# Second attention layer: one transpose of the keys per head, and two ScalarE copies in place of the other

## The chip, the cores and the metric

The kernel runs on one core of one Trainium2 chip. The metric is the device time of one execution in microseconds (us). A core has five engines that run at the same time and wait for each other by semaphores: TensorE (PE in the profile, PEld for its weight loads), VectorE (DVE), ScalarE (ACT), GpSimd (POOL) and SyncE (SP). Each engine works through its own instructions strictly in order. TensorE writes its results to PSUM, eight banks of 128 partitions by 512 float32 columns; the other engines copy them from there to SBUF.

## The reference, cut to what matters

The model is two pre-norm transformer layers on 8 sequences of 512 tokens, width 256. The change lies in the attention of the second layer (L1), which has 16 heads of width 64:

```python
x = x + L0_attn(layernorm(x))
x = x + L0_ffn(layernorm(x))        # mixture of 8 experts
x = x + L1_attn(layernorm(x))       # <- the change is in here
x = x + L1_ffn(layernorm(x))        # fp4-quantised weights and inputs

def _L1_attn_ref(x, W_in, b_in, W_out, b_out):
    proj = x @ W_in.T + b_in                 # q, k, v: 16 heads x 64 each
    q, k = _rope(q, sin, cos), _rope(k, sin, cos)
    att = einsum('bhqd,bhkd->bhqk', q, k) * (1 / sqrt(64))
    att = softmax(where(causal, att, -inf))
    y = einsum('bhqk,bhkd->bhqd', att, v)
    return y @ W_out.T + b_out
```

## The kernel before

L1's attention runs one batch (one sequence of 512 tokens) after the other, eight in all, and in a batch one head after the other. A head's scores are 512 by 512 and causal, so only ten of its sixteen 128x128 tiles are computed. They fall into three groups: the query tiles 0 and 1 (128 and 256 key columns), query tile 2 (384) and query tile 3 (512). One group is one **slot** of the program; slot k of a batch belongs to head k // 3 and group k % 3, so a batch has 48 slots. In this text "the first exponential of a head" is that of its slot 3h, and "the 512-column scores" are those of its slot 3h+2.

Each engine's program is written slot by slot, with a fixed order of parts in a slot and fixed lags in slots behind the scores:

- TensorE (order S, T, P, F): the scores of slot k (S), the transposes of the probabilities of slot k-2 (T), their product with the values of slot k-4 (P), then the fills (F): all work that goes into the two PSUM banks named `W`.
- ScalarE (order P, H, W, E): rounding of projected pieces to float16 (lines 483 to 493), `p_hi`, the float16 half of the transposed probabilities of slot k-2 (H, line 442), copies out of the `W` banks (W, line 453 for the stack, 458 and 474 for others), and at the end the exponential of slot k (E, line 434).
- VectorE (order O, L, W, M, N): head outputs, `p_lo` of slot k-3 (line 538, needs `p_hi`), the projected pieces out of the `W` banks (`t_buf`, line 579, and `rope_u`, line 586), the row maxima of slot k (M, line 531), and the next batch's layer norm.
- GpSimd: the rest of the rotary embedding and the low float16 half of q, k and v (lines 707 to 726).

The scores need float32-like precision, so q and k are each split into a high and a low float16 half of 64 columns, stored side by side in `q_stage` and `k_stage`. Transposed, a query tile has q_hi on partitions 0 to 63 and q_lo on 64 to 127. One matmul against [k_hi; k_lo] gives hi*hi + lo*lo; a second one, against [k_lo; k_hi], gives the cross terms. Both keys' arrangements live in `stack`, 128 partitions by three times 512 columns for each of two heads: queries, keys, keys with their halves swapped. To make the swapped one, `k_stage` holds the high half twice (hi, lo, hi; lines 492 and 493), and TensorE transposes columns 64 to 191 as well.

So the stack of the next head is filled in two parts, `FILLS = 2`. In slot 3h TensorE transposes four query and four key tiles into one `W` bank (line 342), and ScalarE copies 128x1024 out (line 453). In slot 3h+1 TensorE transposes the four swapped key tiles into the other `W` bank, and ScalarE copies 128x512.

The other fills share the two `W` banks in strict turn: 24 pieces of the projection of the next heads (line 371, six matmuls of 512 columns each), four transposes of x, eight of the head outputs (yT), four output projections (proj, float32). A fill waits until the fill two places back has been copied out. Tables give the slots, for instance:

```python
AT_1 = (1, 2, 4, 6, 8, 12, 14, 15, 16, 18, 19, 21)     # pieces, second half of the heads
AT_0 = (24, 26, 28, 30, 33, 34, 36, 38, 39, 40, 42, 43)  # pieces, the next batch's first half
```

The scores of slot k wait for the exponential of slot k-2 (`s_exp`, the two score banks take turns), and those of a head's first slot also for its stack (`s_stev`).

Of the kernel before, what the change touches and what calls it, by code (L numbers as in the profile page):

```python
# [9 lines left out]
ACT = mybir.ActivationFunctionType  # L10
# [4 lines left out]
P = 128  # L15
B, T, D = 8, 512, 256
# [15 lines left out]
K0 = TERMS0 + 8  # L32
# [82 lines left out]
def attention(block, layer, x_sb, stats, consts, w, sem, sb, banks, aside=None):  # L115
# [10 lines left out]
    L1 = layer == 1  # L126
# [9 lines left out]
    DH = DH1 if L1 else DH0  # L136
    HC = P // DH
    CHUNKS = HEADS // HC
    FILLS = 2 if L1 else 1
    QW = 128 if L1 else K0  # L140
    KW = 192 if L1 else K0
    VW = 130 if L1 else 51
    OW = 65 if L1 else 51
    PIECES = 12 if L1 else 4
    S, PT, W, ob = banks[0:2], banks[2:4], banks[5:7], (banks[4], banks[7])
    LOW = F16 if L1 else BF16
# [3 lines left out]
    q_stage = sb(f"q_stage{layer}", [P, 2, QT, 8, QW], LOW)  # L150
    k_stage = sb(f"k_stage{layer}", [P, 2, QT, 8, KW], LOW)
    v_stage = sb(f"v_stage{layer}", [P, 2, QT, 8, VW], LOW)
    stack = sb(f"stack{layer}", [P, 2, (1 + FILLS) * T], LOW)
    xn = sb(f"xn{layer}", [P, 2, D], F32)
    xnT = sb(f"xnT{layer}", [P, 2, C, T] if L1 else [P, C, T], F16 if L1 else F32)
    prob = [sb(f"prob{layer}_{g}", [P, n], F32) for g, n in enumerate(GROUP_COLS)]
# [30 lines left out]
    s_stev = sem("stack_ready")  # L187
# [4 lines left out]
    s_ph = sem("piece_hi_ready")  # L192
# [76 lines left out]
    def _(pe):  # L269
# [57 lines left out]
        def fill(cur, off, kind, *a):  # L327
            b = cur + off
            bank, _ = work_banks.next(kind)
# [4 lines left out]
            if kind == "stack":  # L334
                h, r = a
                if h % 8 == 0 and r == 0:
                    wait(pe, s_piece, (2 * b + h // 8) * PIECES + (8 if L1 else PIECES))
                rows = P if L1 else K0
                pairs = [(q_stage, 0, 0), (k_stage, 0, T)] if r == 0 else [(k_stage, 64, 0)]
                for stage, c0, col in pairs:  # L340
                    for j in range(QT):
                        last = pe.transpose(out.bitcast(LOW)[0:rows, col + j * P:col + (j + 1) * P],  # L342
                                            stage[:, h // 8, j, h % 8, c0:c0 + rows], ident_l[:, :])
                last.then_inc(s_st, 1)
                taken[bank] = (s_stev, FILLS * HEADS, off, FILLS * h + r + 1)
                return
            if kind == "xT":
                j, = a
# [9 lines left out]
            elif kind == "piece":  # L358
                half, p = a
# [64 lines left out]
    def _(act):  # L424
# [19 lines left out]
        def take(kind, b, *a):  # L444
            bank, n = work_banks.next(kind)
            if kind == "stack":
# [1 line left out]
                wait(act, s_st, FILLS * (b * HEADS + h) + r + 1)  # L448
                wait(act, s_scores, 3 * (b * HEADS + h - 1))
                rows = P if L1 else K0  # L450
                dst = stack[0:rows, h % 2, 0:2 * T] if r == 0 else stack[0:rows, h % 2, 2 * T:3 * T]
                src = W[bank][:, :].bitcast(LOW)[0:rows, 0:2 * T if r == 0 else T]
                act.activation(dst, src, ACT.Copy).then_inc(s_stev, 1)  # L453
            elif kind == "xT":
                j, = a
                wait(act, s_fill, n)
# [19 lines left out]
        def piece_hi(b, half, p):  # L476

            m = b * 2 * PIECES + half * PIECES + p
            t, j = piece_parts(p)
            if t == 2:  # L480
                wait(act, s_taken, m + 1)
                wait(act, s_pv, 3 * (b * HEADS - HEADS + 8 * half + 8))
                act.activation(v_stage[:, half, j, :, 0:64], t_buf[:, p % 4, :].rearrange("p (h d) -> p h d", d=64),
                               ACT.Copy).then_inc(s_ph, 1)
                return
            wait(act, s_z, b * 16 + 8 * half + p + 1)
            wait(act, s_st, FILLS * (b * HEADS - HEADS + 8 * half + 8))
            z = rope_z[:, p % 2, :, :]
            if t == 0:
                act.activation(q_stage[:, half, j, :, 0:64], z, ACT.Copy).then_inc(s_ph, 1)  # L490
            else:
                act.activation(k_stage[:, half, j, :, 0:64], z, ACT.Copy)
                act.activation(k_stage[:, half, j, :, 128:192], z, ACT.Copy).then_inc(s_ph, 1)

        def prologue():
            for j in range(QT):
# [2019 lines left out]
```

## Time and profile before

| | |
|---|---|
| median of 3 runs | 2277.01 us (2276.40 to 2287.38) |
| the profiled execution | 2284.02 us, span 2282.2 us |
| mean granted TensorE clock | 0.941 |
| busy: PE, PEld, DVE, ACT, POOL | 1963.1, 1402.1, 1723.2, 1400.1, 1025.3 us |
| prologue and eight batches of L1's attention | about 925 to 1970 us of the span |
| first scores of the eight batches | 970.68, 1109.71, 1233.55, 1355.39, 1477.24, 1599.08, 1720.94, 1843.62 us |

The profile is one execution; its times are not means over runs. A row of the timeline gives the start of an instruction in us from the start of the span, its duration in us, the engine, the line of the kernel, what is written and read, and in brackets how long the engine had been idle before it and what ended the wait. A batch of the middle takes about 121.85 us, and batches 2 to 5 (counted from 0) repeat each other to some hundredths of a microsecond. The worked example of the prediction is batch 3.

### The profile page before, as it was taken

To read this page: it belongs to the slowest core of one execution; us is meant where nothing else is said; L and a number is where in the kernel's file an instruction comes from. 1 tells how busy PE (TensorE), PEld (TensorE's weight loads), DVE (VectorE), ACT (ScalarE), POOL (GpSimd) and SP (SyncE) were. 2 spreads that over 40 slices of the span, in tenths; PEclk is the share of its full clock that TensorE was granted. 3 is DMA by queue.
4 is the path that set the end of the run, shared out by engine and by line. 5 is a ranking of instruction groups with operands and counts; after the bars stand their busy time and mean duration, and the time that the engine had idled before them with its cause. 6 is when DMAs were issued, how large, how long until landed. Compare 5 with 4: busy or idle time off the path is not lost. (4 is left out here: it accounts for less than half of the span.)

```text
span 2282.2 us, 52729 instructions
## 1 busy us (share of the span) xinstructions
PE 1963.1 (86%) x18758; PEld 1402.1 (61%) x18759; DVE 1723.2 (76%) x3728; ACT 1400.1 (61%) x2750; POOL 1025.3 (45%) x1207
## 2 busy tenths in 40 slices
PE   6988999889825996487899999999999999459999
PEld 4666666666623664165677777777767677336665
DVE  8878888888772443487688887878797968679997
ACT  4666666666642443286678786969687879244343
POOL 5434454343032001689757475757675753132222
PEclk9999999999757998799999999999999999769999
DMA  7000000000153332012100000000000000100000
GB/s 245 2 2 2 2 1 2 2 1 2 32 180 90 87 93 62 1 18 36 15 2 2 2 2 1 2 1 2 1 2 2 2 2 2 39 1 16 16 18 24
DMA packets 53369, 57.77 MB, mean 25 GB/s; under 512 B 7104, under 2 KB 47376, under 8 KB 53152
## 3 DMA queue, kind: packets, MB, share of 16 engines
q1 hardware_dynamic: 46528, 45.79, 6.3%
q0 software_dynamic: 6416, 8.95, 1.9%
q8 instruction: 139, 2.28, 0.4%
q14 instruction: 78, 0.64, 0.1%
q10 hardware_dynamic: 208, 0.11, 0.0%
HBM read 36.22 MB, written 18.61 MB: 24 GB/s over the span
## 5 line engine op out<-in xcount | busy, mean ns | idle before, releaser
L371 PE MATMUL a_bank<-w_in_sb,xnT_sb 128*128 128x512 f16 x1152 | 288.6, 389 | 33.8 <-DVE t_buf_sb L579 28.1
L531 DVE TENSOR_REDUCE neg_max_sb<-a_bank 128x1 f32<-128x128 f32 (+3 forms) x512 | 236.0, 482 | 91.4 <-PE a_bank L288 90.0
L1209 DVE TENSOR_REDUCE neg_max_sb<-a_bank 128x1 f32<-128x128 f32 (+3 forms) x512 | 235.9, 484 | 81.7 <-PE a_bank L938 77.6
L1098 ACT ACTIVATE probT_sb<-a_bank 128x512 f32<-128x512 f32 (+1 forms) x384 | 198.7, 526 | 144.4 <-PE a_bank L961 139.5
L442 ACT ACTIVATE p_hi_sb<-a_bank 128x384 f16<-128x384 f32 (+1 forms) x384 | 204.9, 534 | 120.9 <-PE a_bank L297 119.2
L434 ACT ACTIVATE prob_sb<-a_bank,neg_max_sb 128x128 f32<-128x128 f32 (+3 forms) x512 | 260.8, 542 | 22.7 <-DVE neg_max_sb L531 21.8
L538 DVE TENSOR_TENSOR p_lo_sb<-a_bank,p_hi_sb 128x384 f16<-128x384 f32 (+1 forms) x384 | 227.9, 595 | 60.7 <-ACT p_hi_sb L442 57.0
L453 ACT ACTIVATE stack_sb<-a_bank 128x1024 f16<-128x1024 f16 (+1 forms) x256 | 211.1, 825 | 7.1 <-PE a_bank L342 6.7
L297 PE MATMUL a_bank<-ident_f_sb,prob_sb 128*128 128x128 f32 x1280 | 206.9, 277 | 3.7 <-DVE p_lo_sb L538 3.1
L707 POOL TENSOR_TENSOR rope_w_sb<-t_buf_sb,sin_sb 128x256 f32<-128x256 f32 x128 | 146.4, 1144 | 134.6 <-DVE t_buf_sb L579 132.4
L371 PEld LDWEIGHTS a_bank<-w_in_sb,xnT_sb 128*128 128x128 f16 x1152 | 104.1, 99 | 140.6 <-DVE t_buf_sb L579 35.9
L283 PE MATMUL a_bank<-stack_sb 128*128 128x128 f16 (+3 forms) x512 | 148.6, 303 | 26.1 <-ACT prob_sb L434 22.8
L713 POOL TENSOR_TENSOR rope_z_sb<-rope_u_sb,rope_w_sb 128x512 f32<-128x512 f32 x128 | 163.4, 1277 | 10.0
L1396 POOL TENSOR_TENSOR parts_sb<-rest_sb,one_sb 128x256 bf16<-128x256 f32 x60 | 36.7, 612 | 278.2 <-DVE rest_sb L1240 278.2
L318 PE MATMUL a_bank<-v_stage_sb,p_hi_sb 128*128 128x65 f16 x1280 | 159.4, 197 | 0.0
L317 PE MATMUL a_bank<-v_stage_sb,p_hi_sb 128*128 128x65 f16 x1280 | 158.4, 194 | 0.7 <-DVE p_lo_sb L538 0.6
L319 PE MATMUL a_bank<-v_stage_sb,p_lo_sb 128*128 128x65 f16 x1280 | 157.5, 193 | 0.0
L579 DVE SCALAR_TENSOR_TENSOR t_buf_sb<-a_bank,bias_sb 128x512 f32<-128x512 f32 x192 | 131.6, 686 | 33.1 <-PE a_bank L371 21.1
L284 PE MATMUL a_bank<-stack_sb 128*128 128x128 f16 (+3 forms) x512 | 155.0, 303 | 0.0
L297 PEld LDWEIGHTS a_bank<-ident_f_sb,prob_sb 128*128 128x128 f32 x1280 | 135.4, 142 | 30.1 <-issue 4.2
L937 PE MATMUL a_bank<-stack_sb 104*128 104x128 bf16 (+3 forms) x512 | 143.6, 307 | 5.3 <-DVE neg_max_sb L1209 2.9
L2394 POOL TENSOR_TENSOR pair_q_sb<-pair_quot_sb,pair_scale_sb 128x960 f32<-128x960 f32 (+2 forms) x36 | 59.1, 1641 | 197.2 <-DVE pair_quot_sb L2379 197.2
(272 smaller groups left out, 5608.5 us busy)
## 6 DMA issues: line engine op xcount, KB each, us to landing
sorted_rows<-zeros_sb SPq DMA_DIRECT2D x1, 4992.0 KB, 22.7
x_in_sb<-sorted_rows SPq DMA_DIRECT2D x39, 128.0 KB, 2.2
sorted_results<-y_moe_sb SPq DMA_DIRECT2D x39, 128.0 KB, 1.7
x_sb_sb<-L_attn_x SPq DMA_DIRECT2D x8, 512.0 KB, 9.7
w_raw_sb<-L_ffn_gate_bank SPq DMA_DIRECT2D x8, 512.0 KB, 3.8
w_raw_sb<-L_ffn_up_bank SPq DMA_DIRECT2D x8, 512.0 KB, 4.8
w_raw_sb<-L_ffn_down_bank SPq DMA_DIRECT2D x8, 512.0 KB, 5.8
out<-x_sb_sb SPq DMA_DIRECT2D x32, 128.0 KB, 1.7
```

Of the source, the lines that this page charges most:

```text
L297: last = pe.transpose(PT[G_BANK(h, g)][:, n * P:(n + 1) * P], prob[g][:, n * P:(n + 1) * P], ident_f[:, :])
L317: pe.matmul(o, hi, v[:, 0:65], start=a, stop=False)
L318: pe.matmul(o, hi, v[:, 65:130], start=False, stop=False)
L371: last = pe.matmul(out, xnT[:, x, c, j * P:(j + 1) * P], w["in"][:, w_, c, cols], start=k == 0, stop=k == len(terms) - 1)
L434: last = act.activation(prob[g][:, off:off + L], S[(3 * h + g) % 2][:, off:off + L], ACT.Exp, bias=neg_max[:, i:i + 1])
L442: act.activation(p_hi[g][:, h % 2, :], PT[G_BANK(h, g)][:, 0:GROUP_COLS[g]], ACT.Copy).then_inc(s_hi, 1)
L453: act.activation(dst, src, ACT.Copy).then_inc(s_stev, 1)
L531: last = dve.tensor_reduce(neg_max[:, i:i + 1], S[(3 * h + g) % 2][:, off:off + L], AX.X, ALU.max, negate=True)
L538: dve.tensor_tensor(p_lo[g][:, h % 2, :], PT[G_BANK(h, g)][:, 0:GROUP_COLS[g]], p_hi[g][:, h % 2, :], ALU.subtract).then_inc(s_lo, 1)
L713: pool.tensor_tensor(rope_z[:, p % 2, :, :], rope_u[:, p % 2, :, :], rope_w[:, :, :], ALU.add).then_inc(s_z, 1)
L1098: act.activation(probT[:, (h // 4) % 2, h % 4, T_AT[r]:T_AT[r + 1]], ST[(3 * h + r) % 2][:, 0:T_AT[r + 1] - T_AT[r]], ACT.Exp).then_inc(s_ ...
L1209: last = dve.tensor_reduce(neg_max[:, h % 2, i:i + 1], S[(3 * h + g) % 2][:, off:off + L], AX.X, ALU.max, negate=True)
```

## The change

The swapped keys are no longer transposed. `FILLS` becomes 1: TensorE fills one `W` bank per head, and ScalarE copies three times out of it: the 128x1024 copy as before, and then the transposed keys again by 64 partitions, partitions 0 to 63 of PSUM to partitions 64 to 127 of the third part of `stack`, and 64 to 127 to 0 to 63. The third copy releases the stack. `k_stage` is 128 columns wide in place of 192, and its second copy of the high half (line 493) is gone.

```diff
-    FILLS = 2 if L1 else 1
+    FILLS = 1
     QW = 128 if L1 else K0
-    KW = 192 if L1 else K0
+    KW = 128 if L1 else K0
...
-    stack = sb(f"stack{layer}", [P, 2, (1 + FILLS) * T], LOW)
+    stack = sb(f"stack{layer}", [P, 2, (3 if L1 else 2) * T], LOW)
...
                 rows = P if L1 else K0
-                pairs = [(q_stage, 0, 0), (k_stage, 0, T)] if r == 0 else [(k_stage, 64, 0)]
-                for stage, c0, col in pairs:
+                for stage, c0, col in ((q_stage, 0, 0), (k_stage, 0, T)):
                     for j in range(QT):
                         last = pe.transpose(out.bitcast(LOW)[0:rows, col + j * P:col + (j + 1) * P],
...
                 rows = P if L1 else K0
-                dst = stack[0:rows, h % 2, 0:2 * T] if r == 0 else stack[0:rows, h % 2, 2 * T:3 * T]
-                src = W[bank][:, :].bitcast(LOW)[0:rows, 0:2 * T if r == 0 else T]
-                act.activation(dst, src, ACT.Copy).then_inc(s_stev, 1)
+                src = W[bank][:, :].bitcast(LOW)
+                last = act.activation(stack[0:rows, h % 2, 0:2 * T], src[0:rows, 0:2 * T], ACT.Copy)
+                if L1:
+
+                    for a in range(2):
+                        last = act.activation(stack[64 - 64 * a:128 - 64 * a, h % 2, 2 * T:3 * T],
+                                              src[64 * a:64 * a + 64, T:2 * T], ACT.Copy)
+                last.then_inc(s_stev, 1)
...
-                act.activation(k_stage[:, half, j, :, 0:64], z, ACT.Copy)
-                act.activation(k_stage[:, half, j, :, 128:192], z, ACT.Copy).then_inc(s_ph, 1)
+                act.activation(k_stage[:, half, j, :, 0:64], z, ACT.Copy).then_inc(s_ph, 1)
```

On ScalarE, this is what stands from slot 27 to slot 29 of a middle batch (head 9) in the kernel before: the stack copy (L453), the two exponentials of the slot (L434), `p_hi` (L442), the second stack copy, and so on to the exponential of the 512-column slot.

```order
L453 ACTIVATE stack_sb<-a_bank 128x1024
L434 ACTIVATE prob_0_sb<-a_bank,neg_max_sb 128x128
L434 ACTIVATE prob_0_sb<-a_bank,neg_max_sb 128x256
L442 ACTIVATE p_hi_2_sb<-a_bank 128x512
L453 ACTIVATE stack_sb<-a_bank 128x512
L434 ACTIVATE prob_1_sb<-a_bank,neg_max_sb 128x384
L492 ACTIVATE k_stage_sb<-rope_z_sb 128x8x64
L493 ACTIVATE k_stage_sb<-rope_z_sb 128x8x64
L442 ACTIVATE p_hi_0_sb<-a_bank 128x384
L474 ACTIVATE yT_sb<-a_bank 128x512
L434 ACTIVATE prob_2_sb<-a_bank,neg_max_sb 128x512
```

The same place in the changed kernel, whose line numbers differ by a few:

```order
L451 ACTIVATE stack_sb<-a_bank 128x1024
L455 ACTIVATE stack_sb<-a_bank 64x512 x2
L433 ACTIVATE prob_0_sb<-a_bank,neg_max_sb 128x128
L433 ACTIVATE prob_0_sb<-a_bank,neg_max_sb 128x256
L441 ACTIVATE p_hi_2_sb<-a_bank 128x512
L433 ACTIVATE prob_1_sb<-a_bank,neg_max_sb 128x384
L496 ACTIVATE k_stage_sb<-rope_z_sb 128x8x64
L441 ACTIVATE p_hi_0_sb<-a_bank 128x384
L478 ACTIVATE yT_sb<-a_bank 128x512
L433 ACTIVATE prob_2_sb<-a_bank,neg_max_sb 128x512
```

Two copies of 64 partitions now stand ahead of the head's first exponential, the 128x512 copy behind it is gone, and so is the second copy of the key piece.

On TensorE, this is the end of slot 28 and the start of slot 29 in the kernel before: the product with the values (L317 to L319), the four swapped key transposes (L342), a piece of the projection (L371), and the 512-column scores (L283).

```order
L317 MATMUL a_bank<-v_stage_sb,p_hi_0_sb 128x65
L318 MATMUL a_bank<-v_stage_sb,p_hi_0_sb 128x65
L319 MATMUL a_bank<-v_stage_sb,p_lo_0_sb 128x65
L342 MATMUL a_bank<-ident_h_sb,k_stage_sb 128x128 x4
L371 MATMUL a_bank<-w_in_sb,xnT_sb 128x512 x6
L283 MATMUL a_bank<-stack_sb 128x512
```

And in the changed kernel:

```order
L317 MATMUL a_bank<-v_stage_sb,p_hi_0_sb 128x65
L318 MATMUL a_bank<-v_stage_sb,p_hi_0_sb 128x65
L319 MATMUL a_bank<-v_stage_sb,p_lo_0_sb 128x65
L370 MATMUL a_bank<-w_in_sb,xnT_sb 128x512 x6
L283 MATMUL a_bank<-stack_sb 128x512
```

Four transposes are gone between the slot's last product and its piece; nothing else moves on TensorE, and VectorE's and GpSimd's instructions keep their order.

## Rows read from the trace of the kernel before

**Rows 1.** Busy time by stretch: stretch, length, busy us of each engine, clock, DMA.

```profile
1300.00:1400.00 100.00, 97.01 (x1059) 74.44 (x1060) 78.80 (x167) 78.69 (x154) 64.13 (x61) 1.00 0.01 2
```

**Rows 2.** Groups by line and shape: count, busy us, mean ns, idle before.

```profile
L453 ACT ACTIVATE stack_sb<-a_bank 128x1024 f16<-128x1024 f16 x128 | 132.0, 1031 | 7.1 <-PE a_bank L342 6.7
...
L342 PE MATMUL a_bank<-ident_h_sb,k_stage_sb 128*128 128x128 f16 x1024 | 100.3, 221 | 7.4 <-ACT stack_sb L453 7.3
...
L726 POOL TENSOR_TENSOR k_stage_sb<-rope_z_sb,k_stage_sb 128x512 f16<-128x512 f32 x64 | 80.2, 1253 | 11.3 <-ACT k_stage_sb L493 9.8
...
L493 ACT ACTIVATE k_stage_sb<-rope_z_sb 128x512 f16<-128x512 f32 x64 | 40.3, 630 | 0.0
...
L1103 ACT ACTIVATE stack_sb<-a_bank 2x512 bf16<-2x512 f32 x64 | 37.7, 589 | 19.2 <-PE a_bank L947 15.6
```

**Rows 3.** Timeline of TensorE, batch 3, head 9, slots 28 and 29.

```profile
1434.47 0.39 PE L342 MATMUL a_bank<-ident_h_sb,k_stage_sb 128*128 128x128 f16 x4
1434.69 1.46 PE L371 MATMUL a_bank<-w_in_sb,xnT_sb 128*128 128x512 f16 x6
1435.99 0.38 PE L283 MATMUL a_bank<-stack_sb 128*128 128x512 f16 x1
```

**Rows 4.** Timeline of ScalarE, batch 3, slots 27 to 30.

```profile
1433.57 1.02 ACT L453 ACTIVATE stack_sb<-a_bank 128x1024 f16<-128x1024 f16 x1 [0.25 <-PE a_bank L342]
1434.49 0.72 ACT L434 ACTIVATE prob_sb<-a_bank,neg_max_sb 128x128 f32<-128x128 f32 x2
1435.09 0.61 ACT L442 ACTIVATE p_hi_sb<-a_bank 128x512 f16<-128x512 f32 x1
1435.57 0.62 ACT L453 ACTIVATE stack_sb<-a_bank 128x512 f16<-128x512 f16 x1
1436.05 0.61 ACT L434 ACTIVATE prob_sb<-a_bank,neg_max_sb 128x384 f32<-128x384 f32 x1
...
1438.40 0.74 ACT L434 ACTIVATE prob_sb<-a_bank,neg_max_sb 128x512 f32<-128x512 f32 x1
...
1439.35 1.08 ACT L453 ACTIVATE stack_sb<-a_bank 128x1024 f16<-128x1024 f16 x1
```

**Rows 5.** Timeline of VectorE, batch 3, slots 28 and 29.

```profile
1435.73 0.69 DVE L538 TENSOR_TENSOR p_lo_sb<-a_bank,p_hi_sb 128x512 f16<-128x512 f32 x1 [0.34 <-ACT p_hi_sb L442]
1436.34 0.68 DVE L579 SCALAR_TENSOR_TENSOR t_buf_sb<-a_bank,bias_sb 128x512 f32<-128x512 f32 x1
1437.05 0.69 DVE L586 TENSOR_TENSOR rope_u_sb<-t_buf_sb,cos_sb 128x512 f32<-128x512 f32 x1
1437.66 0.68 DVE L531 TENSOR_REDUCE neg_max_sb<-a_bank 128x1 f32<-128x512 f32 x1
```

**Rows 6.** Timeline, batch 3: first exponential, then 512-column scores, of heads 8 and 10.

```profile
1428.42 0.74 ACT L434 ACTIVATE prob_sb<-a_bank,neg_max_sb 128x128 f32<-128x128 f32 x2
1429.37 0.38 PE L283 MATMUL a_bank<-stack_sb 128*128 128x512 f16 x1
...
1440.27 0.78 ACT L434 ACTIVATE prob_sb<-a_bank,neg_max_sb 128x128 f32<-128x128 f32 x2
...
1441.77 0.38 PE L283 MATMUL a_bank<-stack_sb 128*128 128x512 f16 x1
```

**Rows 7.** The same pair of heads 12 and 13 of batch 3.

```profile
1454.35 0.74 ACT L434 ACTIVATE prob_sb<-a_bank,neg_max_sb 128x128 f32<-128x128 f32 x2
...
1455.15 0.39 PE L283 MATMUL a_bank<-stack_sb 128*128 128x512 f16 x1 [0.23 <-ACT prob_sb L434]
...
1460.47 0.73 ACT L434 ACTIVATE prob_sb<-a_bank,neg_max_sb 128x128 f32<-128x128 f32 x2
...
1463.41 0.38 PE L283 MATMUL a_bank<-stack_sb 128*128 128x512 f16 x1
```

**Rows 8.** The same pair of head 14 of the last batch.

```profile
1936.78 0.73 ACT L434 ACTIVATE prob_sb<-a_bank,neg_max_sb 128x128 f32<-128x128 f32 x2
...
1937.56 0.39 PE L283 MATMUL a_bank<-stack_sb 128*128 128x512 f16 x1 [0.41 <-ACT prob_sb L434]
```

## The prediction

> **What bounds the kernel now.** I read the busy times by stretch first. In the steady batches TensorE is busy 97.0 of 100 us at the full granted clock, VectorE 78.8, ScalarE 78.7 and GpSimd 64.1 [rows 1]. So TensorE looks like the bound, and work taken off it looks like a gain; but a busy share tells nothing of who waits in a loop. Next I read the timeline of one head on three engines [rows 3 to 5]. TensorE's own work of head 9, from its 512-column scores (1435.99) to those of head 10 (1441.77), takes 5.78 us [rows 3, 6]. The same 5.78 us is the distance of the two stack copies on ScalarE, 1433.57 and 1439.35 [rows 4]. The way between these copies is an unbroken chain over two engines: stack copy 1433.57, exponentials 1434.49, `p_hi` 1435.09, then VectorE's `p_lo` at 1435.73, which had waited 0.34 us for `p_hi`, the piece out of its bank 1436.34, the rotary product 1437.05, the row maximum 1437.66, then back to ScalarE's exponential at 1438.40 and, two instructions later, the next stack copy [rows 4, 5]. In a head with little projection work this loop is as long as TensorE's work: ScalarE and VectorE have slack on average, but not on this path.
>
> Third, the distance from the end of a head's first exponential to the 512-column scores that need it. Heads 8, 9, 10 and 12 have 0.21, 0.78, 0.72 and 0.06 us (1428.42 + 0.74 = 1429.16 against 1429.37, and so on), head 13 has 2.21 [rows 3, 4, 6, 7]. It must be at least 0.06, as where TensorE is shown to wait for it [rows 7]. The long ones have two pieces of projection, or an output projection, between the stack's fill and these scores; the short ones have one piece or none.
>
> **The change part by part.** *TensorE* loses four transposes a head, 512 of the 1024 in the key group [rows 2]. The group of four starts at 1434.47 and the next work at 1434.69: 0.22 us [rows 3] (the busy times of single matmuls overlap and can't be added). For 128 heads that is 28.2 us, if TensorE is the bound at each.
>
> *ScalarE* gains two 64x512 copies ahead of the first exponential and loses the 128x512 copy behind `p_hi`. No row shows a copy from one half of the partitions to the other. The nearest, 128x512 from the same bank, takes 0.48 us from its start to that of the next instruction (1435.57 to 1436.05) [rows 4]; the 128x1024 copy takes 0.92 (1433.57 to 1434.49) [rows 4]. Whether half the rows halve the price is answered best by a copy of 2 partitions by 512, whose mean is 589 ns, against 619 for the 128x512 copy at 1435.57 [rows 2, 4]: rows hardly count. I take 0.5 us for each, 1.0 for both. Bounds: 0.25 each if rows did count, 0.62 each if the copies did not overlap at all.
>
> The Trainium skill, page "ScalarE: Activation LUTs", section "What ACT_TABLE_LOAD costs", has one element per cycle and lane, 186 ns + 0.833 ns for each element of the row, and 93 ns of overlap; by it the estimate is 1.04 us for both copies, and no less for half the partitions. By that the sum below would stand about 2 us higher; the two-partition row agrees with it.
>
> *The first exponential ends 1.0 us later.* Behind it on ScalarE are `p_hi` of the slot before, the exponentials of the head's other two slots, and rounding of pieces; TensorE's 512-column scores wait for it. Where the distance is over 1.0 + 0.06, nothing is lost and the 0.22 is won. Where it is d, the scores come 1.0 - (d - 0.06) later: 0.28 in head 9, 0.85 in head 8, 1.0 in head 12.
>
> *The loop.* `p_hi` is delayed by the same 1.0 us, and the removed copy stands behind it, so it gives nothing back here. In head 9, `p_lo`, piece, rotary product, maximum and the last exponential follow without a gap [rows 5], so the next stack copy starts 1.0 later, and with its own two small copies head 10's first exponential ends 2.0 later. Its distance is 0.72: head 10's 512-column scores are 1.34 late, of which 0.28 were counted in head 9. With 0.08 more at the next wait this makes 1.14 for head 10.
>
> *One batch.* I went through the 16 heads of batch 3 in this way, starting at head 4, since the output projections before it leave ScalarE idle and reset the loop. Gain or loss of each in us: head 4 +0.28, 5 -0.22, 6 and 7 +0.07 together (VectorE is busy without a gap there on the next batch's layer norm and sets the pace), 8 +0.84, 9 +0.28, 10 +1.14, 11 +0.05, 12 +0.83, 13 -0.39, 14 +0.04, 15 +1.20, then head 0 +0.11, 1 +0.37, 2 +0.88 (the late maximum delays the copy of yT, whose bank a piece waits for), 3 -0.42. The larger gains of 13 and 3 are bank waits that go, since one fill a head less takes its turn. The losers sum to +6.09, the winners to -1.03: **+5.1 us a batch**.
>
> *The second copy of the key pieces* (630 ns [rows 2]) goes; in the steady batches ScalarE's next instruction mostly waits for TensorE or VectorE anyway, so I give it nothing there; were that cover gone, 64 copies at 0.52 would be worth up to 33 us. In the prologue GpSimd waits for it (9.8 us in all behind line 493 [rows 2]): four pieces at about 0.52 make -2.1, and the extra copy before the first scores +0.5: -1.6.
>
> *The sum.* Six middle batches: 6 x 5.1 = 30.6. First batch: its second half like the others +4, its first half, where GpSimd sets part of the pace, an estimate of +2: 6. Last batch: its second half has no projection work, the scores wait for the first exponential in each head (1936.78 + 0.73 = 1937.51 against 1937.56 [rows 8]); seven heads lose between 0.5 (ScalarE's net work) and 1.0, I take 0.7, 4.9; its first half 1.9. Together 30.6 + 6 + 6.8 - 1.6 = **+41.8 us** on the profiled execution's 2284.0, so 2325.8. That execution stands 7.0 us above the median of the runs, so on the median's scale 2277.0 + 41.8 = **2319 us**, 1.8% slower.
>
> **The rivals.** All on the median's scale.
>
> *A: the copies are hidden everywhere.* Then -28.2 - 1.6: 2247 us. For it: TensorE's 97.0 against ScalarE's 78.7. Against: the distances of 0.06 to 0.78. It decides below about 0.4 us for both copies, where the ledger's losers sink to the size of the winners. [...]
>
> *B: the wait is direct only.* If VectorE takes the late `p_lo` in its stride, the heads lose only what the first wait costs: in the ledger +1.9 a batch, 11.4 for six, with 6 for the first and last together less 1.6: 2293 us. For it: VectorE's 78.8. Against: the gapless rows of head 9.
>
> *C: the loop closes in every head.* Each pays 1.0 - 0.22: 128 x 0.78 = 100, 2377 us. Against: head 13's 2.21 us and the idle ScalarE during the output projections.
>
> *D: a copy of half the partitions takes half the time.* The exponential is 0.5 late, ScalarE's net work is zero, and the ledger nearly cancels, about +0.7 a batch: 2283 us with the ends. Against: the 2-partition row.
>
> **How the numbers follow.** Chances: forecast 0.50, B 0.20, C (or most of it) 0.10, D 0.12, A 0.08. The predicted time is the forecast's. Copies of 0.62 us each would add about 0.24 at nine losing heads, 2 us a batch, 16 in all; errors of the ledger of 2 us a batch are as much: 2300 to 2337 for the forecast alone. The range reaches from D, 2283, to 2352, where it leaves out A and the upper part of C. About 0.5% (11.4 us) is what a measurement of this kernel can tell from no change. Forecast, B and C are slower than that: 0.80. D is within: 0.12. A is faster: 0.08.
>
> **What would show it.** Right: small copies that start 0.5 us apart; the first exponential's end to the 512-column scores at 0.06 in heads 8, 9, 10, 12, 15 and all heads of the last batch's second half; a distance about 1.2 us smaller in the long heads; middle batches of about 127 us against 121.85; TensorE's busy share down, and its idle time ahead of the scores put down to the exponential; GpSimd no longer waiting behind line 493. Wrong: middle batches under 121 us (A), of 122 to 124 (B, D), with the spacing of the small copies telling D from B, or above 130 (C).

## The result and the profile after

The changed kernel took 2359.68 us (median of four runs, 2355.82 to 2362.29) against 2277.85 for the kernel before on the same chip (2276.40 to 2287.38): ratio 1.0329, 95% interval 1.0300 to 1.0358. It is slower, by 82 us where 42 were forecast. All ratios here are of fast runs; one of the ten runs of e2 took 3973.93 us and is not in its ratio. The profiled execution took 2362.29 us with a span of 2360.5; its span is 78.3 above that of before, and the numbers below are read from these two traces.

The period of a batch, from the first scores of one batch to those of the next, shows where the time went. Before, the seven periods were 139.03, 123.84, 121.84, 121.85, 121.85, 121.85 and 122.69 us; after, 142.98, 133.45, 131.53, 131.68, 131.53, 132.12 and 131.71. From the last batch's first scores to the start of the feed-forward part it took 133.18, now 150.50. So the first batch lost 3.9, the six middle ones 58.1 together, the last 17.3; 1.6 were won ahead of the first scores.

Busy time by stretch, in the columns of [rows 1], the same 100 us:

```profile
1300.00:1400.00 100.00, 84.27 (x946) 61.83 (x943) 79.85 (x165) 85.49 (x161) 62.77 (x60) 1.00 0.01 2
```

These 100 us are less than a batch and hold other heads of it in each kernel, so 97.0 and 84.3 can't be compared. Here is a whole batch, batch 3, first before, then after:

```profile
1355.39:1477.24 121.85, 116.38 (x1281) 88.42 (x1282) 99.89 (x209) 96.61 (x189) 77.21 (x72) 1.00 0.01 2
...
1377.01:1508.69 131.68, 116.51 (x1219) 86.88 (x1218) 101.23 (x210) 105.17 (x197) 77.43 (x73) 0.98 0.01 2
```

TensorE has fallen from 95.5% of the batch to 88.5%, VectorE from 82.0 to 76.9, and ScalarE went from 79.3 to 79.9. No engine is nearer its limit than before, and TensorE is still the busiest. Something that no busy share shows, a chain over several engines, sets the pace.

The groups that answer to [rows 2], whole span:

```profile
L455 ACT ACTIVATE stack_sb<-a_bank 64x512 f16<-64x512 f16 x256 | 151.5, 592 | 3.0
...
L451 ACT ACTIVATE stack_sb<-a_bank 128x1024 f16<-128x1024 f16 x128 | 131.2, 1025 | 15.1 <-PE a_bank L341 14.5
...
L729 POOL TENSOR_TENSOR k_stage_sb<-rope_z_sb,k_stage_sb 128x512 f16<-128x512 f32 x64 | 80.3, 1254 | 10.3 <-ACT k_stage_sb L496 10.3
...
L341 PE MATMUL a_bank<-ident_h_sb,k_stage_sb 128*128 128x128 f16 x512 | 52.2, 227 | 0.0
```

Half the key transposes are gone. A copy of half the rows lasts 592 ns, against 619 for the 128x512 copy of before. GpSimd still waits 10.3 us behind the copy of the key pieces.

The two ends of the loop, as in [rows 4, 5]: head 9 of batch 3 on ScalarE, then on VectorE.

```profile
1459.72 1.02 ACT L451 ACTIVATE stack_sb<-a_bank 128x1024 f16<-128x1024 f16 x1 [0.33 <-PE a_bank L341]
1460.76 1.20 ACT L455 ACTIVATE stack_sb<-a_bank 64x512 f16<-64x512 f16 x2
1461.98 0.73 ACT L433 ACTIVATE prob_sb<-a_bank,neg_max_sb 128x128 f32<-128x128 f32 x2
1462.60 0.60 ACT L441 ACTIVATE p_hi_sb<-a_bank 128x512 f16<-128x512 f32 x1
...
1465.88 0.69 ACT L433 ACTIVATE prob_sb<-a_bank,neg_max_sb 128x512 f32<-128x512 f32 x1 [0.74 <-DVE neg_max_sb L534]
...
1466.84 1.03 ACT L451 ACTIVATE stack_sb<-a_bank 128x1024 f16<-128x1024 f16 x1
```

```profile
1463.23 0.69 DVE L541 TENSOR_TENSOR p_lo_sb<-a_bank,p_hi_sb 128x512 f16<-128x512 f32 x1 [1.68 <-ACT p_hi_sb L441]
1463.84 0.68 DVE L582 SCALAR_TENSOR_TENSOR t_buf_sb<-a_bank,bias_sb 128x512 f32<-128x512 f32 x1
1464.56 0.69 DVE L589 TENSOR_TENSOR rope_u_sb<-t_buf_sb,cos_sb 128x512 f32<-128x512 f32 x1
1465.16 0.68 DVE L534 TENSOR_REDUCE neg_max_sb<-a_bank 128x1 f32<-128x512 f32 x1
```

From the 128x1024 copy to the first exponential it is 2.26 us, where [rows 4] have 0.92: 1.34 more. From one stack copy to the next it is 7.12, where it was 5.78: 1.34 more. In this head the whole delay goes round the loop once and comes out at its end. VectorE's wait for `p_hi` has grown from 0.34 to 1.68, by 1.34 again, and behind it the four instructions follow each other as before.

What TensorE and VectorE waited for between 1250 and 1850 us (line waited for: us in total, times, longest):

```profile
PE a_bank L283 <- ACT prob_sb L433: 37.1, 42, 2.5
...
PE a_bank L370 <- ACT stack_sb L455: 5.8, 13, 0.6
...
DVE p_lo_sb L541 <- ACT p_hi_sb L441: 65.2, 56, 2.9
```

In the same stretch before, TensorE's wait for the exponential was 6.6 us in 20 times, and VectorE's for `p_hi` 23.8. The second row is new: the matmuls of a piece need the bank that the third copy releases.

First exponential and 512-column scores, as in [rows 3, 7, 8]: head 9 of batch 3 by the exponential above (1461.98 + 0.73 = 1462.71, scores at 1462.77), then heads 8 of batch 3 and 14 of the last batch.

```profile
1454.73 0.73 ACT L433 ACTIVATE prob_sb<-a_bank,neg_max_sb 128x128 f32<-128x128 f32 x2
1455.52 0.39 PE L283 MATMUL a_bank<-stack_sb 128*128 128x512 f16 x1 [1.25 <-ACT prob_sb L433]
...
2018.39 0.73 ACT L433 ACTIVATE prob_sb<-a_bank,neg_max_sb 128x128 f32<-128x128 f32 x2
...
2019.18 0.39 PE L283 MATMUL a_bank<-stack_sb 128*128 128x512 f16 x1 [1.98 <-ACT prob_sb L433]
```

The distance is 0.06 in both, with TensorE idle for 1.25 and 1.98 us before it.

### The profile page after: what moved, and what is told of

Read it like the earlier page. It is cut to its first block and busy times, and to the rows that moved or that the text cites. A ratio compares the mean times of both kernels' runs of the same rounds, so it can differ in the third digit from the quotient of the medians.

```text
span 2360.5 us, 51642 instructions
## 1 busy us (share of the span) xinstructions
PE 1962.3 (83%) x18246; PEld 1389.1 (59%) x18247; DVE 1730.3 (73%) x3728; ACT 1468.8 (62%) x2814; POOL 1025.7 (43%) x1207
## 5 line engine op out<-in xcount | busy, mean ns | idle before, releaser
L370 PE MATMUL a_bank<-w_in_sb,xnT_sb 128*128 128x512 f16 x1152 | 294.0, 394 | 42.2 <-ACT stack_sb L455 17.8
L283 PE MATMUL a_bank<-stack_sb 128*128 128x128 f16 (+3 forms) x512 | 151.0, 307 | 90.5 <-ACT prob_sb L433 87.9
L317 PE MATMUL a_bank<-v_stage_sb,p_hi_sb 128*128 128x65 f16 x1280 | 160.0, 195 | 0.7 <-DVE p_lo_sb L541 0.6
L319 PE MATMUL a_bank<-v_stage_sb,p_lo_sb 128*128 128x65 f16 x1280 | 159.3, 194 | 0.0
L455 ACT ACTIVATE stack_sb<-a_bank 64x512 f16<-64x512 f16 x256 | 151.5, 592 | 3.0
```

Source lines behind the costliest of these rows:

```text
L317: pe.matmul(o, hi, v[:, 0:65], start=a, stop=False)
L319: last = pe.matmul(o, lo, v[:, 0:65], start=False, stop=z)
L370: last = pe.matmul(out, xnT[:, x, c, j * P:(j + 1) * P], w["in"][:, w_, c, cols], start=k == 0, stop=k == len(terms) - 1)
```

## The experiments

Theories. *Loop and price*: the loss is what ScalarE adds between the stack copy and the first exponential, times the heads in which the loop or the direct wait closes. *Direct wait only*: VectorE takes the late `p_hi` in its stride. *Length*: ScalarE's additional microsecond a head costs wherever it stands. *Bank*: the loss is the bank that is held longer. All ratios are to the kernel before, run on the same chip with the kernel named; edits are against the changed kernel. e1, e2 and e3 leave out the product's terms that need the swapped halves of the keys: the stack holds unswapped ones there. One fill fewer for each head, and with it another turn of the two `W` banks, is in all twelve, also in e2 and e7, which are not slower.

**e1: two 128x512 copies.** As long in sum as the ledger assumed, in the same place.

```diff
-                    for a in range(2):
-                        last = act.activation(stack[64 - 64 * a:128 - 64 * a, h % 2, 2 * T:3 * T],
-                                              src[64 * a:64 * a + 64, T:2 * T], ACT.Copy)
+                    act.activation(spare[:, :], src[:, T:2 * T], ACT.Copy)
+                    last = act.activation(stack[:, h % 2, 2 * T:3 * T], src[:, T:2 * T], ACT.Copy)
```

> The two 64-row copies are replaced by two 128x512 copies of the transposed keys (one into a spare tile, one unswapped into the third part of the stack, so the cross terms of the scores are left out). The distance from the start of the 128x1024 copy to that of the first exponential, 0.92 us before and 2.26 us in the changed kernel, should be about 1.9 here. Theory 'price' (the ledger is right, only the two copies cost 1.34 us in place of 1.0): about 2319 us, 2305 to 2333, so half of the loss. Theory 'ledger' (at 1.0 us the loop closes in more heads than I followed): 2340 us or more.

Measured: 2319.45 us, ratio 1.0154 (1.0120 to 1.0188). ScalarE's timeline:

```profile
1461.21 1.02 ACT L452 ACTIVATE stack_sb<-a_bank 128x1024 f16<-128x1024 f16 x1
1462.11 0.61 ACT L455 ACTIVATE spare_sb<-a_bank 128x512 f16<-128x512 f16 x1
1462.59 0.62 ACT L456 ACTIVATE stack_sb<-a_bank 128x512 f16<-128x512 f16 x1
1463.07 0.76 ACT L434 ACTIVATE prob_sb<-a_bank,neg_max_sb 128x128 f32<-128x128 f32 x2
```

Each instruction starts before the one ahead of it has ended, by about 0.13 us: 1.86 from the first to the exponential, 0.94 more than before. Batches 2 to 5 took 126.6 us, 4.7 more than before; the ledger had 5.1 at a price of 1.0. By the ratio e1 is 35 us slower, where the forecast had 42; that its 2319 is also the forecast's number is chance, since the kernel before ran 2286 on this chip.

**e2: one 128x512 copy** in place of the two.

```diff
-                    for a in range(2):
-                        last = act.activation(stack[64 - 64 * a:128 - 64 * a, h % 2, 2 * T:3 * T],
-                                              src[64 * a:64 * a + 64, T:2 * T], ACT.Copy)
+                    last = act.activation(stack[:, h % 2, 2 * T:3 * T], src[:, T:2 * T], ACT.Copy)
```

> One 128x512 copy in place of the two 64-row ones (unswapped, so the cross terms of the scores are left out): 0.5 us ahead of the first exponential, as one copy less behind p_hi. Theory 'price': the losses and gains of the heads nearly cancel, about 2283 us, 2270 to 2295. Theory 'ledger': the losers still lead, 2300 us or more.

Measured: 2284.64 us, ratio 1.0002 (0.9985 to 1.0019); middle batches 122.9. At half the price gain and loss cancel, as rival D had worked out.

**e3: the same halves, not crossing.**

```diff
-                        last = act.activation(stack[64 - 64 * a:128 - 64 * a, h % 2, 2 * T:3 * T],
+                        last = act.activation(stack[64 * a:64 * a + 64, h % 2, 2 * T:3 * T],
```

> The two 64-row copies stay on their own half of the partitions (unswapped, so the cross terms of the scores are left out). If a copy does not overlap its neighbours because it crosses from one half of the partitions to the other: 128x1024 copy to first exponential 1.9 us and about 2319 us. If because its rows start at another partition than its neighbour's: one or two of the three overlaps stay lost, 2.1 to 2.26 us and 2340 to 2360 us.

Measured: 2347.11 us, ratio 1.0271 (1.0235 to 1.0307).

```profile
1457.73 1.02 ACT L451 ACTIVATE stack_sb<-a_bank 128x1024 f16<-128x1024 f16 x1 [0.33 <-PE a_bank L341]
1458.65 1.18 ACT L455 ACTIVATE stack_sb<-a_bank 64x512 f16<-64x512 f16 x2
1459.85 0.73 ACT L433 ACTIVATE prob_sb<-a_bank,neg_max_sb 128x128 f32<-128x128 f32 x2
```

The first copy, which reads and writes the lower half, starts 0.92 behind the stack copy and overlaps it. The pair and the exponential behind it do not overlap (1.18 and 1.20 for the two): 2.12 in all. So of the 0.40 by which the changed kernel's copies cost more than those of e1, 0.26 go with the split into halves and 0.14 with the crossing.

**e4 and e5: the copies later.** In e4 they stand behind the head's first exponentials, ahead of `p_hi`; in e5 behind that `p_hi`. Their source is still the bank, which only the last of them releases.

```diff
+            while held:
+                h, src = held.pop()
+                for a in range(2):
+                    last = act.activation(stack[64 - 64 * a:128 - 64 * a, h % 2, 2 * T:3 * T],
+                                          src[64 * a:64 * a + 64, T:2 * T], ACT.Copy)
+                last.then_inc(s_stev, 1)
```

> The two 64-row copies stand behind the first exponentials of the head instead of ahead of them, still ahead of p_hi. If the direct wait of the 512-column scores for the first exponential makes the loss: about 2255 to 2285 us. If the way over p_hi, p_lo, row maximum and the last exponential to the next stack copy makes it: 2310 us or more, with the scores waiting for the second and third exponential and for the stack.

> The two 64-row copies stand in slot 3h+1 behind p_hi, where the 128x512 copy of the kernel before stood. Neither the first exponential nor p_hi is late then. If the loop over p_hi is what costs (theory 'loop'): most of the loss is gone, 2265 to 2295 us; what is left is that a W bank is held until the third copy, so a piece in slot 3h+1 waits for it. If ScalarE's longer work as such costs (0.7 us a head net): 2330 us or more.

Measured: e4 2354.14 us, ratio 1.0307 (1.0279 to 1.0336); e5 2376.75, ratio 1.0392 (1.0372 to 1.0413). Taking the direct wait of the head's own exponentials away (e4) gives back about 5 us, within the intervals nothing, but the bank is now held longer: TensorE's waits for these copies grew from 6.4 to 26.2 us. The expectation for e5 was missed by 80. Its waits on TensorE, 1250 to 1850 us:

```profile
PE a_bank L370 <- ACT stack_sb L449: 46.7, 35, 1.9
PE a_bank L387 <- ACT stack_sb L449: 16.3, 10, 1.6
```

The wait for the exponential is down from 37.1 to 13.5, but 63 us of waits for the held bank came in its place. Two causes are mixed here, so e9 to e11 separate them.

**e6: four transposes put back** on TensorE (the key's, made a second time into the same place).

```diff
-                for stage, c0, col in ((q_stage, 0, 0), (k_stage, 0, T)):
+                for stage, c0, col in ((q_stage, 0, 0), (k_stage, 0, T)) + (((k_stage, 0, T),) if L1 else ()):
```

> The changed kernel with four more key transposes a head (the transposed keys are written a second time to the same place of the bank), so that TensorE has its old work again. If TensorE's time is no longer on the path where ScalarE's loop sets the pace, at most 12 us above the changed kernel, 2360 to 2372; if it still sets the pace, 28 us more, 2388.

Measured: 2373.61 us, ratio 1.0373 (1.0351 to 1.0396), 0.0044 above the changed kernel's: about 10 us, with 8 either way, by the two intervals. Of the 28.2 us of the saved transposes about a third, by the intervals between 2 and 18 us, still reached the changed kernel's time.

**e7: the halves swapped by two DMAs** from SyncE's queue, so that ScalarE does no swap at all.

```diff
+                for a in range(2):
+                    sp.dma_start(stack[64 - 64 * a:128 - 64 * a, G % 2, 2 * T:3 * T],
+                                 stack[64 * a:64 * a + 64, G % 2, T:2 * T]).then_inc(s_oev, 16)
...
+                    wait(pe, s_oev, 32 * (b * HEADS + h + 1))
```

> The halves are swapped by two DMAs from SBUF to SBUF, issued by SyncE behind the 128x1024 copy, so ScalarE does no small copies and TensorE no second transposes. If the loop through ScalarE set the pace: faster than before, 2250 to 2265 us, if the swapped keys land within the some 3 us that a short head leaves from the end of the copy to the next head's first scores. If they land later, the scores wait for them: 2280 us or more with a wait on a DMA.

Measured: 2272.74 us, ratio 0.9940 (0.9919 to 0.9962): 0.6% faster than the kernel before. On the scale of the expectation (2250 to 2265) the ratio gives 2264. Middle batches 119.3 us. Busy time of one of them:

```profile
1225.47:1344.73 119.26, 112.13 (x1217) 84.94 (x1217) 100.45 (x209) 85.87 (x165) 77.10 (x72) 1.00 0.08 19
```

TensorE is back at 94.0% with the shorter work. The batch is 2.6 us shorter than before: that is what the single transpose is worth once the swap is off the loop, together with the two ScalarE copies, of the stack and of the key piece, that are gone here too; the two were not separated. The DMA issues between 1250 and 1850 us (count, KB each, median us from issue to landing):

```profile
stack_sb<-stack_sb SPq DMA_DIRECT2D x160, 64.0 KB, 2.0
```

Half of them land within 2.0 us of their issue, the slowest took 3.7, and a head lasts about 7. TensorE waited for a landing nine times in this stretch, 4.2 us in all.

**e8: the second copy of the key pieces restored** to the changed kernel.

```diff
+                act.activation(k_stage[:, half, j, :, 128:192], z, ACT.Copy).then_inc(s_ph, 1)
```

> The changed kernel with the second ScalarE copy of the key pieces' high half put back (k_stage of 192 columns, the extra 64 unused). The prediction gave that copy 2.1 us in the prologue and nothing in the batches: 2360 to 2365 us. If ScalarE's work in the loop counts in full, 64 x 0.52 = 33 us more: 2393.

Measured: 2380.14 us, ratio 1.0397 (1.0375 to 1.0419), 0.0068 or about 15 us above the changed kernel, with 8 us either way; middle batches 133.4 against 131.7. That lies between the two expectations. The first and last key piece of the prologue on GpSimd, in the kernel before and in the changed one:

```profile
937.23 1.16 POOL L726 TENSOR_TENSOR k_stage_sb<-rope_z_sb,k_stage_sb 128x512 f16<-128x512 f32 x1 [1.26 <-ACT k_stage_sb L493]
...
966.62 1.16 POOL L726 TENSOR_TENSOR k_stage_sb<-rope_z_sb,k_stage_sb 128x512 f16<-128x512 f32 x1 [1.26 <-ACT k_stage_sb L493]
```

```profile
936.43 1.15 POOL L729 TENSOR_TENSOR k_stage_sb<-rope_z_sb,k_stage_sb 128x512 f16<-128x512 f32 x1 [0.74 <-ACT k_stage_sb L496]
...
964.26 1.15 POOL L729 TENSOR_TENSOR k_stage_sb<-rope_z_sb,k_stage_sb 128x512 f16<-128x512 f32 x1 [0.74 <-ACT k_stage_sb L496]
```

From first to last it is 29.39 and 27.83 us, and 29.41 in e8 (941.08 to 970.49): GpSimd's wait is 0.52 shorter at each piece, and three of them make the 1.56. In the steady batches the removed copies were worth 1.7 us a batch in the changed kernel. The other 4.7 us by which e8's prologue starts later lie ahead of it, in work that the edit doesn't touch.

**e9, e10, e11: place and bank apart.** The copies read the stack, so that the first copy releases the bank by itself; the scores wait for the two copies. e9: behind `p_hi`, where the kernel before had its second stack copy. e10: behind the first exponentials, ahead of `p_hi`. e11: in the changed kernel's own place. The edit of all three; only where `swap()` is called differs:

```diff
+                n, r = held.pop()
+                wait(act, s_stev, n + 1)
+                for a in range(2):
+                    last = act.activation(stack[64 - 64 * a:128 - 64 * a, r, 2 * T:3 * T],
+                                          stack[64 * a:64 * a + 64, r, T:2 * T], ACT.Copy)
+                last.then_inc(s_oev, 1)
...
+                act.activation(stack[0:rows, h % 2, 0:2 * T], src[0:rows, 0:2 * T], ACT.Copy).then_inc(s_stev, 1)
+                held.append((b * HEADS + h, h % 2))
```

> The two 64x512 copies take the first copy's result in the stack as their source and stand behind the first rounding copy in slot 3h+1; the first copy releases the bank by itself and the scores wait for the two copies. Theory loop (the copies cost because they stand between the stack copy, the exponentials and the rounding copy that the key blocks wait for): the loop is that of before, TensorE keeps its 0.22 a head, 2255 to 2290. Rival length (ScalarE 1.3 us longer in each head costs wherever it stands): 2330 or more. If only the held bank cost in the earlier run with this place, the 2377 of that run falls below 2300.

> The same source, the copies behind the first exponentials and ahead of the rounding copy: no wait of the head's own exponentials for them, and no bank held, but the loop keeps them. Theory loop: 2315 to 2345. If the held bank was the cost of the run with this place and the bank as source (2354): 2290 or less.

> The same source in the changed kernel's own place, ahead of the exponentials: loop and direct wait stay, only the bank is free 1.2 us sooner. Theory loop: 2340 to 2365, at most 15 below the changed kernel, since the waits for the bank behind the copies are 5.8 us of 600 there. If the bank was the cost: 2310 or less. If copies that read the stack overlap each other as the 128-row ones do, their price falls towards 1.0 and the time towards 2320.

Measured: e11 2374.79 us, ratio 1.0405 (1.0369 to 1.0441); e10 2343.43, 1.0267 (1.0232 to 1.0303); e9 2299.46, 1.0075 (1.0043 to 1.0107). The same two copies, of the same length, cost 92, 61 or 17 us by the place alone: 31 us go with the direct wait of the head's own exponentials, 44 more with `p_hi`. e9 lies 9 us above its expectation. In e11 nothing was won by the free bank; it fell outside its expectation, on the slow side. ScalarE in e11:

```profile
1384.00 1.02 ACT L463 ACTIVATE stack_sb<-a_bank 128x1024 f16<-128x1024 f16 x1
1385.06 1.27 ACT L451 ACTIVATE stack_sb<-stack_sb 64x512 f16<-64x512 f16 x2
1386.35 0.73 ACT L434 ACTIVATE prob_sb<-a_bank,neg_max_sb 128x128 f32<-128x128 f32 x2
```

Copies out of the stack are longer, and the first of them has to wait for the end of the 128x1024 copy: 2.35 to the exponential, 0.09 above the changed kernel. In e9 the copies are behind `p_hi`, and the second exponential stands behind them:

```profile
1387.96 0.60 ACT L442 ACTIVATE p_hi_sb<-a_bank 128x512 f16<-128x512 f32 x1 [2.79 <-PE a_bank L298]
1388.58 1.27 ACT L451 ACTIVATE stack_sb<-stack_sb 64x512 f16<-64x512 f16 x2
1389.87 0.58 ACT L434 ACTIVATE prob_sb<-a_bank,neg_max_sb 128x384 f32<-128x384 f32 x1
```

**e12: one step further back**, behind the second exponential.

```diff
                     exp(b, k // 3, k % 3)
+                    if L1 and k % 3 == 1:
+                        swap()
```

> The same stack source; the two copies stand one step further back than in e9, behind the head's second exponential (128x384) and ahead of the next rounding copy. Theory loop: like e9 they are outside the loop of stack copy, first exponentials, rounding copy and key blocks, so the time stays far below the changed kernel: 2260 to 2310. What is left in e9 (1.6 a batch above the kernel before) is then put down to the second exponential behind the copies, and goes if it is that alone: 2255 to 2285; it stays or grows (2290 to 2320) if the rounding copy and the third exponential behind the new place are as close to TensorE's wait. Rival length (ScalarE's 1.3 a head costs wherever it stands): 2330 or more.

Measured: 2315.10 us, ratio 1.0130 (1.0092 to 1.0167). Not better than e9: the rest isn't the second exponential alone. TensorE's waits, 1250 to 1850 us:

```profile
PE a_bank L284 <- issue: 21.5, 38, 1.1
...
PE a_bank L284 <- ACT stack_sb L451: 8.9, 5, 1.8
PE a_bank L284 <- ACT prob_sb L434: 5.7, 14, 0.6
```

The wait for the exponential is nearly gone (26.1 us in e9), but the next head's scores now wait for the copies themselves. That is the second row, and the first too, which has no releaser in the view: each of its 38 matmuls starts 0.10 us after the end of a second copy of the pair. Together they make 30.4 us. None of the four places that were tried was free of cost.

**Together.** Added time between the stack copy and the first exponential, and the time of the kernel, with the copies in the changed kernel's place:

```
kernel    added us   ratio    ratio x 2280 us, above before
e2          0.48     1.0002       0
e1          0.94     1.0154     +35
e3          1.20     1.0271     +62
after       1.34     1.0329     +75
e11         1.43     1.0405     +92
```

From e1 to the changed kernel 0.40 us add 40, from e1 to e11 0.49 add 57: 100 to 116 us for one microsecond, with some 25 either way by the intervals. If each of the 128 heads paid all of it, it would be 128. So past about 1 us most heads pay.

## Why the prediction was right or wrong

**The bound.** Right. It was the loop and not TensorE's 97.0% (95.5% over a whole batch). With 28 us of work off TensorE and 1.34 us a head into the loop, all of it showed up at the loop's end in head 9; that [rows 3] and [rows 4] had the same 5.78 was the sign. The Trainium skill's page "Perfetto Trace Analysis", section "Identifying the Most-Contended Engine", says that the busy share of the matmuls is no good measure of how near TensorE is to its limit, and names the share of the peak matmul rate and the busy share of the weight loads in its place. The trace agrees: the engine with 97.0 was relieved and the kernel got slower, and the weight loads had 74.4 in [rows 1], below VectorE's 78.8 and ScalarE's 78.7. A's time came near only when the swap left ScalarE (e7, 2273), and there 13 us were won where A had 30.

**The price of the two copies: here the prediction failed.** The step read "I take 0.5 us for each, 1.0 for both". They cost 1.34, and e1, with copies that cost 0.94 in the same place, lost 35 us in place of 75. The 1.34 come from 1.04 behind the 128x1024 copy (0.92 before), then 0.60 and 0.62. Even the upper bound, 0.62 each, left out that the copy ahead of them loses its own overlap of 0.1. The sources stood in [rows 2, 4]: the row of 2 partitions was read for its duration, and the spacing for the small copies was taken from the 128-row copy, of which 0.13 lies under the next instruction. The start-to-start time of small copies was in the trace of before, in the layer ahead:

```profile
300.28 1.02 ACT L1118 ACTIVATE stack_sb<-a_bank 104x1024 bf16<-104x1024 bf16 x1 [0.59 <-PE a_bank L994]
301.20 0.59 ACT L1098 ACTIVATE probT_sb<-a_bank 128x512 f32<-128x512 f32 x1
...
305.06 0.59 ACT L1103 ACTIVATE stack_sb<-a_bank 2x512 bf16<-2x512 f32 x1 [0.64 <-PE a_bank L947]
305.68 0.87 ACT L1098 ACTIVATE probT_sb<-a_bank 128x512 f32<-128x512 f32 x2
```

The copy of 104 rows from partition 0 gives 0.1 of its time to the next instruction; the copy of 2 rows, which starts at partition 96, gives nothing. The Trainium skill, page "ScalarE: Activation LUTs", section "What ACT_TABLE_LOAD costs", states 93 ns of overlap, by which the estimate was 1.04 for both. e1 comes near it (0.94, with overlaps of 0.11 to 0.14 in its trace); the copies of halves, which didn't overlap, don't.

**What a microsecond in the loop costs: mis-sized too.** "Copies of 0.62 us each would add about 0.24 at nine losing heads", 16 us: 67 for a microsecond. The runs show 100 to 116. At its own 67 the missing 0.34 would have given 23 us more, 2342; the other 18 are this rate. It is higher because more heads than nine lie in the loop once the first 1.0 us has used up their distances, and because the last batch and stretches of lower clock add to it. By head, from the starts of successive 512-column scores in the middle batches, where the clock stayed up: with 0.40 more in the loop than e1, heads 0, 1, 4, 8, 9 and 10 take 0.37 longer each, 7 and 15 0.69 and 0.51, 11, 12 and 14 0.20 to 0.24; only 2, 5 and 13 pay 0.12 or less, and 3 and 6 nothing. Together 4.3 a batch, as much as 11 of the 16 heads paying all of the 0.40.

**The ledger.** Right at its own price. e1 has +4.7 a batch for +5.1. By head it is right in heads 2 to 5 and 9 to 11 (head 9 +0.26 for +0.28, head 10 +0.96 for +1.14, head 3 -0.44 for -0.42). It is wrong by 0.9 too high in heads 6 and 7 together, 1.3 too low in head 8, 0.9 too high in head 0 and 0.5 too low in head 15. These errors cancel, so it is in part luck that the sum of the batch came out.

**Middle batches.** 58.1 for 30.6. The higher price accounts for those 4.3 a batch, 26 us, less the 0.4 a batch by which the ledger was too high. The rest, some 4 us, goes with the granted clock, which the prediction took as constant: in three of the batches head 0 took 1.3 to 1.4 longer than in the others, behind a stretch of lower clock.

**First batch and prologue.** 3.9 for an estimate of 6. The prologue's parts were right: on GpSimd it takes 34.5 us from the start of the first query piece (932.11) to that of the last key piece (966.62) before and 32.4 after (931.83 to 964.26), so four pieces gave the 2.1 of the forecast. From there to the first scores it takes 0.7 longer, for +0.5. The total of -1.6 agrees, with 0.3 won ahead of these pieces; by itself it would show little, since the first scores start anywhere from 961 to 975 in the traces of the twelve experiments.

**Last batch.** 17.3 for 6.8. The distances of 0.06 came in each head from 7 to 14, as forecast; the price was 0.9 to 1.6 a head for 0.7, and two heads lost 3.0 and 2.5. From one head's scores to the next, ending with heads 10, 11 and 13:

```profile
1984.80:1992.84 8.04, 6.06 (x64) 5.09 (x65) 4.02 (x9) 5.95 (x12) 0.00 (x0) 0.79 0.01 3
1992.84:1998.78 5.94, 3.96 (x60) 3.42 (x61) 3.73 (x9) 5.46 (x11) 0.00 (x0) 1.00 0.00 0
...
2005.20:2012.76 7.56, 5.58 (x60) 4.67 (x61) 4.00 (x9) 5.46 (x11) 0.00 (x0) 0.77 0.00 0
```

The two long ones are those with a clock of 0.79 and 0.77; TensorE is busy for 1.6 to 2.1 us longer in them than in the short one.

**The second copy of the key pieces.** "I give it nothing there" was too low: e8 shows 1.7 us a batch in the changed kernel. That GpSimd would no longer wait there was right for this copy and wrong for the sum: it waits 10.3 us, where it was 9.8 [rows 2], behind the copy that stayed. What it was worth in the kernel before was not tried.

**What was to be seen.** The small copies start 0.60 apart for 0.5. The distance is 0.06 in heads 8, 9, 10, 12 and 15, as forecast; in the long heads 2, 3, 6 and 13 it shrank by 1.4 to 2.2 for 1.2; the price of 1.34 in place of 1.0 accounts for 0.34 of that. TensorE's share fell and its largest wait is the one for the exponential.

**The rivals.** B (direct wait only) falls by e4, where the direct wait is gone and 3.07% of the 3.29% stay, and more cleanly, with the bank free in both, by e10, where 61 of the 92 us of e11 stay. C (every head) overrates it: it gave 100 at a price of 1.0, and e1 has 35. D had its arithmetic right (e2), but the copy of half the rows isn't half as long. The theory of length falls by e9 to e11 for all but the 17 us of e9: the same length costs 17 or 92 us. That of the bank falls by e11, but the bank explains e5 (2377) against e9 (2299).

**Open.** Why ScalarE's halves don't overlap is not settled: e3 takes the crossing away and keeps the split, and only its first copy overlaps. How much of e9's remaining 17 us is ScalarE's own length was not separated.

## What to carry to other kernels

Price an instruction by the distance from its start to the next start, in a row of its own kind (rows, first partition, memory), not by its duration nor by a wider sibling: here 0.12 us of overlap, three times a head, doubled the loss. When two engines' chains have the same length as the bound's work, price the loop by the turn, times the turns in which it closes, and expect their number to grow with the price; a copy's place in the loop decided between 17 and 92 us. And if data only has to change partitions and there are 2 us to spare, give it to a DMA queue that has nothing else to do (e7).

## What the hardware showed that was not expected

Overlap on ScalarE was lost by copies of half of the partitions. 128-row copies out of a bank started 0.48 apart at 0.62 long (e1), copies of 64 rows out of a bank 0.60 apart at 0.59 (after) and copies of 64 rows out of the stack 0.64 apart at 0.63 (e9). In e4 a 64-row copy overlapped what followed where that read another memory (0.50 to the rounding of a piece out of the stage's buffers) and not where it read a bank (0.62). The copies out of the stack show the reverse (e10, e12; medians of the starts from 1250 to 1850 us): 0.53 to `p_hi`, which reads a bank, and 0.65 to the rounding of a piece. The exponentials, which read a bank and the row maxima, overlapped neither kind (0.62 and 0.65). So in these runs a 64-row copy overlapped what followed only where the two had no memory to read in common; whether that is the cause was not tested.

TensorE's clock fell behind some stretches of idle time and not behind others. Two-microsecond windows of batch 3 after:

```profile
1439.00:1441.00 2.00, 0.17 (x6) 0.04 (x2) 1.93 (x5) 0.56 (x2) 0.00 (x0) 1.00 0.00 0
1441.00:1443.00 2.00, 1.78 (x27) 1.75 (x27) 2.00 (x6) 1.35 (x3) 0.00 (x0) 0.80 0.00 0
1443.00:1445.00 2.00, 2.00 (x13) 1.19 (x11) 1.90 (x4) 1.74 (x3) 1.12 (x1) 0.50 0.00 0
```

TensorE stood still for 2.05 us from 1439.17; then the granted clock fell to 0.50, the lower of its two levels, 1.2 GHz. Six matmuls of a piece took 2.39 us there against 1.47 at 2.4 GHz. The next head gave 0.6 us of that back. From 1250 to 2020 us TensorE stood still 17 times for 1.98 us or longer. Behind eight of these stretches the clock fell to 0.50, behind nine it stayed at 1.00, among them the same place of batches 2 and 4 (2.05 us up to 1310.34 and 1573.56); no fall came without one. What decides was not found. In the kernel before the same middle batches ran at 0.99 to 1.00; in e5 four of them ran at 1.00 and took 133.5 us each, longer than the changed kernel's. So the waits don't need the lower clock; it adds to them.
